# Feed-forward steps between attention rounds: the products with w2 of one job set stand among the products with w1 and w3 of the next, in the banks of the value products

## The reference

```python
def _swiglu(h, w1, w2, w3):
    return silu(h @ w1.T) * (h @ w3.T) @ w2.T
...
# layer 0: x -> x + attention + feed-forward, xn = layernorm(x)
d2 = maximum(q2[..., :, None] + k2[..., None, :] - 2.0 * qk, 1e-12)   # 16 heads of 8
attn = softmax(-sqrt(d2)); out = (attn @ v) @ wo.T + bo
shared_out = _swiglu(xn, sw1, sw2, sw3)                               # 352 wide
probs = sigmoid(clip(xn @ router_w.T + routing_bias, -50, 50))        # top 1 of 7 experts
switched = sum over e of where(sel == e, p, 0) * _swiglu(xn, ew1[e], ew2[e], ew3[e])
out = 0.5 / total_weight * shared_out + switched / total_weight
# layer 1: softmax attention, and sqrt(real * real + imag * imag) of two products
```

## Time and profile before

| | us |
|---|---|
| median of 3 runs (lowest, highest) | 1550.39 (1549.52, 1551.34) |
| the profiled execution's own time | 1553.23 |
| its span in the profile | 1551.5 |
| ACT busy | 1450.2 (93% of the span) |
| DVE busy | 1273.7 (82%) |
| PE busy | 1131.7 (73%) |
| POOL busy | 421.4 (27%) |

### The profile page before, as it was taken

The page is one execution under the profiler, slowest core; times in us unless marked ns, Lnnn a source line. Parts: engine busy times, 40 slices in busy tenths (PEclk is TensorE's granted clock), DMA queues, the critical chain, the costliest instruction groups (busy, mean ns, idle before and its releaser), DMA issues.

```text
span 1551.5 us, 21372 instructions
## 1 busy us (share of the span) xinstructions
PE 1131.7 (73%) x7849; PEld 441.9 (28%) x7876; DVE 1273.7 (82%) x2285; ACT 1450.2 (93%) x798; POOL 421.4 (27%) x273
## 2 busy tenths in 40 slices
PE   4587777788548788788788774877677677676665
PEld 2123223234104424334234231142122222221212
DVE  6997888988648898897987968956898889897886
ACT  3899999999629999999999999998999999999997
POOL 5274450230732131230330330043123114022200
PEclk8598998999769999999999987889999999999999
DMA  4842544211122421221221412133033133021001
GB/s 113 240 125 67 160 128 111 66 43 48 43 61 57 138 62 41 53 61 30 66 50 41 95 44 53 27 106 79 26 107 82 29 107 80 26 101 33 23 29 55
DMA packets 104035, 112.71 MB, mean 73 GB/s; under 512 B 41699, under 2 KB 76003, under 8 KB 103923
## 3 DMA queue, kind: packets, MB, share of 16 engines
q1 hardware_dynamic: 98202, 98.63, 23.3%
q0 software_dynamic: 4464, 11.09, 2.6%
q10 hardware_dynamic: 1256, 1.53, 0.4%
HBM read 66.52 MB, written 44.70 MB: 72 GB/s over the span
## 4 chain that ended last, share of the span: by engine, by line
ACT 62%; DVE 14%; PE 12%; issue 10%; DMA 1%; another core or an unknown queue 1%; ACTq 0%; SPq 0%; DVEq 0%
ACT scores L628 22%; ACT scores L617 20%; ACT exp L1143 13%; DVE scores L592 6%; DVE exp L1150 4%; PE pvb L573 3%; ACT exp L1139 3%; PE ring L1119 2%; PE ring L558 2%; PE ring L838 2%; ACT L628 1%; ACT ht L877 1%; ACT L617 1%; PE ring L858 1%
## 5 line engine op out<-in xcount | busy, mean ns | idle before, releaser
L592 DVE TENSOR_SCALAR scores<-ring 128x1024 f32<-128x1024 f32 x512 | 589.9, 1215 | 59.6 <-remote 34.6
L617 ACT ACTIVATE scores<-scores 128x8192 f32<-128x8192 f32 x60 | 417.4, 7021 | 45.8 <-DVE scores L592 45.7
L628 ACT ACTIVATE scores<-scores 128x8192 f32<-128x8192 f32 x64 | 445.8, 7020 | 0.2
L1143 ACT ACTIVATE exp<-ring 128x1024 f32<-128x1024 f32 x428 | 414.6, 1270 | 9.7 <-PE ring L1119 9.7
L573 PE MATMUL pvb<-scores,val 128*9 128x256 f32 x4096 | 334.2, 397 | 99.4 <-issue 57.2
L1119 PE MATMUL ring<-stk 128*128 128x512 bf16 x997 | 303.7, 386 | 141.1 <-ACT exp L1143 108.9
L1150 DVE SCALAR_TENSOR_TENSOR exp<-exp 128x512 f32<-128x512 f32 x428 | 329.7, 794 | 63.5 <-ACT exp L1143 59.6
L558 PE MATMUL ring<-stk 64*128 64x512 bf16 x1024 | 212.5, 412 | 77.5 <-DVE scores L592 62.2
L1119 PEld LDWEIGHTS ring<-stk 128*128 128x128 bf16 x1024 | 62.1, 97 | 357.9 <-ACT exp L1143 262.8
L558 PEld LDWEIGHTS ring<-stk 64*128 64x128 bf16 x1024 | 49.9, 94 | 314.3 <-DVE scores L592 218.2
L573 PEld LDWEIGHTS pvb<-scores,val 128*9 128x9 f32 x4096 | 67.4, 89 | 234.0 <-issue 229.5
(11 more groups left out here) (240 smaller groups left out, 1180.9 us busy)
## 6 DMA issues: line engine op xcount, KB each, us to landing
stk<-stack SPq DMA_DIRECT2D x190, 192.0 KB, 2.9
stack<-qp SPq DMA_DIRECT2D x7, 768.0 KB, 4.4
stack<-kp SPq DMA_DIRECT2D x7, 768.0 KB, 3.8
xj<-xg SPq DMA_DIRECT2D x10, 448.0 KB, 4.2
yg<-yj POOLq DMA_DIRECT2D x10, 448.0 KB, 3.6
stack<-qp SPq DMA_DIRECT2D x7, 512.0 KB, 5.1
stack<-kp SPq DMA_DIRECT2D x7, 512.0 KB, 4.9
stk<-sum_rows SPq DMA_DIRECT2D x126, 24.0 KB
```

Of the source, the lines that this page charges most:

```text
L592: nc.vector.tensor_scalar(S[place][:, j * N:(j + 1) * N], tile, 1e-12, None, ALU.max).then_inc(o.release(("qk", group, place, j)), 1)
L617: nc.scalar.activation(S[place][:], S[place][:], ACT.Sqrt).then_inc(root_done, 1)
L628: nc.scalar.activation(S[place][:], S[place][:], ACT.Exp, scale=-1.0).then_inc(exp_done, 1)
L1143: nc.scalar.activation(EX[i // 2][:, i % 2, :], tile, ACT.Exp, scale=SCALE1).then_inc(o.release(("qk1", n, i)), 1)
```

## The change

The products with w2 no longer take a ring tile. They go to the two banks `pvb`, four tiles to the first and three to the second, and are issued tile by tile between the products with w1 and w3 of the next set: down 0, then down 1 and up 0, down 2 and up 1, and so on to down 6 and up 5, then up 6. For this PE waits, before the first of them, until the last divide of the round has read the banks (`att_ready`), and the values product of the next round waits at places 0 and 1 until `yj` has been copied (slot `AUX`). DVE copies the result with two instructions, one for each bank, now behind the seven tiles of w1 and w3. The semaphore `down_done` takes the place of the ring's.

```diff
+    def begin_apart(self, pe, key, slot):
+
+        if self.turn[slot]:
+            pe.wait_ge(self.free[slot], self.turn[slot])
+        self.of[key] = (None, slot, self.turn[slot])
+        self.turn[slot] += 1
...
-        def pe_values0(pe, group, place, j):
+        def pe_values0(pe, o, group, place, j):
...
                 elif group:
                     pe.wait_ge(att_ready, GROUP * (group - 1) + place + 3)
+                    if FIRST_JOBS < group <= LAST_JOBS + 1:
+                        o.emptied(pe, ("down", group - 1))
...
-        def pe_down(pe, o, v, e):
-            tile = o.begin(pe, ("down", v))
-            o.emptied(pe, ("hidden", v, PAIRS_OF_JOBS - 1))
-            for j in range(JOBS):
-                for c in range(3):
...
+        def pe_down(pe, o, v, j, e):
+
+            if j == 0:
+                o.begin_apart(pe, ("down", v), AUX)
+            if j % 2 == 0:
+                o.emptied(pe, ("hidden", v, j // 2))
+            at_col = j % 4 * P
+            for c in range(3):
+                width = min(P, I - c * P)
+                mm = nc.tensor.matmul(pvb[j // 4][:, at_col:at_col + P], ht[0:width, j, c * P:(c + 1) * P],
...
+            if j == JOBS - 1:
+                mm.then_inc(down_done, 1)
+
+        def pe_jobs(pe, o, r, e_down, e_up):
+
+            for j in range(JOBS + 1):
+                if j < JOBS and FIRST_JOBS < r <= LAST_JOBS + 1:
+                    pe_down(pe, o, r - 1, j, e_down)
+                if j and FIRST_JOBS <= r <= LAST_JOBS:
+                    pe_up(pe, o, r, j - 1, e_up)
...
         def dve_keep_down(dve, o, v):
-            tile = o.filled(dve, ("down", v))
+            dve.wait_ge(down_done, v - FIRST_JOBS + 1)
             dve.wait_ge(y_stored, 16 * (v - FIRST_JOBS))
-            nc.vector.tensor_copy(yj[:, :, :], tile[:, 0:JOBS * P].rearrange("p (j c) -> p j c", c=D)
-                                  ).then_inc(o.release(("down", v)), 1)
+            for i, n in enumerate((4, JOBS - 4)):
+                last = nc.vector.tensor_copy(yj[:, 4 * i:4 * i + n, :],
+                                             pvb[i][:, 0:n * P].rearrange("p (j c) -> p j c", c=D))
+            last.then_inc(o.release(("down", v)), 1)
...
-                    if FIRST_JOBS < r <= LAST_JOBS + 1:
-                        pe_down(pe, o, r - 1, e_down)
-                    if FIRST_JOBS <= r <= LAST_JOBS:
-                        pe_up(pe, o, r, e_up)
+                    if r > FIRST_JOBS:
+                        pe.wait_ge(att_ready, GROUP * r)
+                    pe_jobs(pe, o, r, e_down, e_up)
...
+                    if FIRST_JOBS <= r <= LAST_JOBS:
+                        dve_keep_up(dve, o, r)
                     if FIRST_JOBS < r <= LAST_JOBS + 1:
                         dve_keep_down(dve, o, r - 1)
-                    if FIRST_JOBS <= r <= LAST_JOBS:
-                        dve_keep_up(dve, o, r)
```

49 lines of the change are left out of this document (24 added, 25 removed).

## The result

| | before | with the change |
|---|---|---|
| median, us | 1550.39 (1547.57 to 1555.29, 5 runs) | 1563.79 (1557.25 to 1565.51, 5 runs) |
| profiled execution, own time / span, us | 1553.23 / 1551.5 | 1557.25 / 1555.5 |

The ratio of the times is 1.0082, with a 95% interval of 1.006 to 1.0103. The kernel became 13.4 us slower, where 4.7 us was forecast. So its trace need not show all that the median pays for. Two later executions of the same kernel, traced in the experiments, show what this one does and one thing more.

The account below looks back on a forecast made before the run. ACT was taken to bound the kernel, with DVE and PE under 2 us ahead; 1.5 us (gaps after rounds 4 and 5) plus 3.2 (rounds 7 to 13) gave +4.7, a median of 1555.1 us, range 1549.5 to 1562.0.

Parts of the forecast that it names:

- The new wait, the cost: After a gap, the values product waits for `yj` and the first distance follows: 1.05 us, bounds 0 to 1.6.
- rival C: PE restarts at the low clock after gaps, 1.8 us each; at one gap in three 1558.7 us; chance 0.12.
- rounds 7 to 14: Forecast for rounds 7 to 13: DVE's cycle of 60.9 us exceeds ACT's 60.37, costing 3.2 us (0.5 to 7.4).
- Gaps after rounds 4 and 5: only the copies count.: DVE's placing there hides PE's restart, so only the late copies cost: 0.6 and 0.9 us, 1.5 in sum.
- The gap: Between rounds: 16.4 us from the end of the token transposes, making DVE's cycle 60.9 us (60.45 to 61.6).
- Round 5: ACT's wait for DVE in round 5 would grow from 1.61 us to some 2.2 us.
- The first up tile: In the gap, it would not be held, since `xjt` is copied while two down tiles (1.4 us) run first.
- Rival A: Down's weight loads pass under the up products, saving 3.1 us a gap: 1547.8 us; chance 0.08.
- Rival D: Round 6's placing stretch gains or loses one waiting tile, 11.5 us more or less; chance 0.06, half each side.
- Round 6: The late copies in the gap after round 5 would add 0.9 us, on the path because ACT waits in round 6.
- Parts at nothing: `att_ready` wait, tanh, POOL's `yj` store, SP's queue, one ring tile less, gaps after rounds 3 and 13: no cost.
- The profiled execution: Forecast to rise by 4.7 us, from its own time of 1553.23 us to 1557.9.

Follow-up runs that it names:

- e8: The changed kernel with the placing after rounds 4 and 5 moved ahead of the up tiles on DVE: 1516.35 us against 1514.73, ratio 1.0013.
- e9: The kernel before the change, with only the placing moved ahead of the copy to `yj` on DVE: 1506.11 us against 1514.73, ratio 0.9937.
- e1: The changed kernel timed once more, unaltered, against the kernel before: 1561.19 us against 1549.61, ratio 1.0075.
- e12: The changed kernel timed a third time, unaltered, against the kernel before: 1564.56 us against 1548.17, ratio 1.0103.
- e5: The changed kernel with 8 instead of 11 placing steps after round 4 and 3 more after round 5: 1530.69 us against 1514.74, ratio 1.0118.
- e2: The changed kernel with the w2 products in one block again, ahead of those with w1 and w3, copies still last: 1563.25 us, ratio 1.0082.
- e6: The changed kernel with PE making the next round's first three distance tiles ahead of the values product: 1525.76 us against 1514.74, ratio 1.0085.

## Why the prediction was wrong in size

The direction, the place and the chain were right. Two steps failed. In the one traced execution that is taken apart below they add 10.5 us to the forecast, and round 6, where ACT waited less instead of more, takes 2.5 us off.

1. **"The new wait, the cost": 1.05 us from `yj` to the first distance copy.** It was 1.88 us, plus 0.29 before the second, in five gaps of seven, and 1.24 us in the two with the full clock. Of this 0.2 us is the release, which I put at 0.06 and which measured 0.25 (615.86 to 616.11). The rest is the clock. It was in rival C, with a chance of 0.12 and at one gap in three. I had the 2.3 us of idling right (2.44) and beside it a row with the low clock after 4.97 us, and should have made the restart at the low clock the forecast. Even the upper bound that I had set for this wait, 1.6 us at the low clock, was passed. Its price of 1.8 us a gap was too high: it measured 1.0 us, since only the first two distances are late, not four. In sum, rounds 7 to 14 cost 8.5 us instead of 3.2, with the parted roots, which I had not counted, in it for 1.0. Without any collision, and on a chip where round 6 covers nothing, the change costs 10.2 us (e8 against e9), twice the forecast.

2. **"Gaps after rounds 4 and 5: only the copies count."** I held the placing as the cover of PE's restart and asked what it hides, not what it would run into. Before, placing ended 0.9 us ahead of POOL's product (the distances follow at 329.15, the product begins at 330.03). With the change it ended 0.7 us later after G (24.97 us against 24.31), and in the first execution 0.5 us was left (329.89 and 330.39). In the other two DVE was later against ACT even before this gap: G of round 4 comes 20.86 and 20.68 us after ACT's first root of the round, against 19.82 in the first execution and 20.11 in the kernel before. So the copies brought the collision within reach, and 0.9 to 1.0 us of difference between executions made it. Where that comes from stays open. In two executions of three this costs 5.6 us in ACT's waits of round 5 (7.6 against 1.99). The sign stood in the trace of before, a step of 38 elements that took 5.26 us after round 5 and ended within 0.03 us of POOL's product. The best evidence is the same kernel with the collision (e1, e12) and without it, and then e5, in which the collision left round 4 and doubled after round 5 when three steps were moved. In all the traces 12 DVE instructions of placing took 4.8 us and more. Each of them began within one of these POOL products and ended within 0.1 us of its end. e8 and e9 fit but move the placing out of the path as well.

The Trainium skill (SBUF — State Buffer, "Who interferes with whom") has the rule: DVE and GpSimd share a pair of SBUF ports, and whichever instruction starts first holds the pair to its end. It counts among DVE's claimants an instruction with two SBUF inputs, against a GpSimd instruction that reads SBUF, and a copy, a cast or a scalar step in a two-port mode (one that reads a single operand through both ports), but no reduction. The traces agree: the two-input step took 5.1 us more than usual, the cast 4.7 to 5.1, the scalar step 4.6 to 5.1, and the reduction at 393.31, well inside POOL's product, its usual 0.42. The other way round, where DVE's two-input step began 0 to 0.12 us first, POOL's product took 0.1 to 0.3 us more. That the cast and the scalar step ran in a two-port mode no trace shows. The rule bore on this change, and I had not weighed it.

Put together for the execution of e1, the first that had both: the roots of round 6 begin 6.2 us later than before (413.38 against 407.19), the waits of round 6 take 1.6 back (42.4 against 44.05 us), and rounds 7 to 14 add 8.0 (7.1 of waits, the rest the parted roots). That is the 12.6 us by which the roots of round 15 are later (1003.15 against 990.55), near the 11.6 us of e1's medians and the 13.4 of the first ones. The forecast had 0.6, 0.9 more and 3.2 for these three.

The other steps:

- *The gap.* The tokens end at G + 5.65 (6.2 taken), down and up take 13.4 us from there (13.1), the last up tile 1.04 (1.05), the copies 1.15 (1.2), the restart 1.88 (1.05), and from there to the next G it is 38.7 (38.3). The sum is 61.8 us, against 60.9 forecast and 61.6 as its upper end. The early tokens took back 0.5 us of what the rest cost. At the full clock the cycle is 60.82. That this is the forecast's 60.9 is in part luck: the tokens came 0.45 us earlier, down and up took 0.2 longer and the restart 0.2.
- *Round 14*, thought free, cost a wait of 0.6 us.
- *Round 5.* The wait is 1.99 us without the collision, 2.2 was forecast.
- *The first up tile*, said not to be held, waits for `xjt` in six of the seven gaps, 0.08 to 0.17 us.
- *PE's idling before.* The values product waited up to 1.11 us by the rows that I read. After round 11 it was 1.57 us.
- *Rival A.* Down and up did not get shorter but 0.3 to 0.4 us longer. Down's loads keep PEld busy for 54.7 us instead of 47.6, with 9.5 us idle before them instead of 6.0, and those of up for 49.5 instead of 53.2. Both together it is 104.2 us, against 100.8, so no load time was saved by passing under the longer products:

```profile
L870 PEld LDWEIGHTS pvb<-w,ht 128*128 128x128 f32 (+1 forms) x420 | 54.7, 191 | 9.5
```
- *Rival D.* The long wait of round 6 went from 38.3 us to 37.0, 36.7 and 36.7 in the three executions. It neither grew nor fell by 11.5.
- *Round 6*, put at 0.9 us more, cost 1.6 us less in ACT's waits. A later DVE did not make them longer, and why is open.
- *Parts at nothing.* The tanh, POOL's store of `yj` and the wait for `att_ready` show no wait of ACT, nor does the ring's tile less.
- *The profiled execution.* That of the change came out 4.0 us above that of before, close to the forecast of 4.7. This is by chance: 8.5 us in rounds 7 to 14 instead of 3.2, less 0.9 by which it came earlier to round 7, less 3.6 of difference behind round 15's first root.

## What to carry to other kernels

Before a copy is moved behind a block, ask who waits behind the copy, how long that engine will have been idle, and at what clock it restarts: here 1.15 us of copies, the wait behind them and the low clock made a round up to 1.4 us longer. And look at each short DVE instruction that lasts as long as a POOL instruction beside it. It may be held, and if a change moves DVE by 1 us, count which of these meetings it makes or ends. Placing these instructions where DVE waits for PE anyway gave 0.6% in the kernel before.

## What the runs showed of the hardware

- A two-input, cast or scalar instruction of DVE on SBUF operands that began inside a POOL product of 5.4 to 5.7 us took 4.8 to 5.3 us instead of 0.16 to 0.18, in 12 cases of 12. Five reductions that began inside one took their usual 0.39 to 0.42. Where a two-input DVE instruction began 0 to 0.12 us ahead of POOL's product, it took its usual 0.42 us and the product 5.56 to 5.70 instead of 5.4 to 5.5, in four cases. Copies out of PSUM are not held: the eight distance copies after round 4 began at 337.95 in the third execution of the change, took 9.13 us, and POOL's second product ran from 338.09 beside them.
- After 2.44 us of idling, the first product of PE ran at the low clock, wholly or in part, in five gaps of seven in each of two executions of the change, in four of seven in the third (e12), in seven of seven in the block version with the copies last (e2), and at the full clock in the others. With the idle time filled (e6) the restart was at the full clock and the transposes of six gaps of seven were slower instead.
- Interleaving products of 128 columns with products of 352 made both together 0.4 us longer in 13.1, of which 0.17 is a wait for DVE.
- The same kernel takes 1550 us on some chips and 1515 on others. In the traces the difference lies in round 6, where ACT's longest wait for DVE is 33.5 to 38.3 us on the ones and at most 5.4 on the others.
